# A late pair of normalisations behind the first GELU, and a split of x moved behind two tiles, in a conditional MLP

## The reference

```python
out_nr  = gelu(x @ w1_nr  + b1_nr)  @ w2_nr  + b2_nr      # condition 0
out_tsr = gelu(x @ w1_tsr + b1_tsr) @ w2_tsr + b2_tsr     # condition 1
h = gelu(x @ w1_sr + b1_sr)                               # condition 2, hidden size 1024
h = gelu(h @ w2_sr + b2_sr)
out_sr = h @ w3_sr + b3_sr
y = x + where(c == 0, out_nr, where(c == 1, out_tsr, where(c == 2, out_sr, 0)))
return (y - mean(y)) * rsqrt(var(y) + 1e-5) * gamma + beta
```

## Time and profile before

| | us |
|---|---|
| median of three runs | 562.37 (561.03 to 562.45) |
| the profiled execution's own time | 561.57 |
| span of the profiled execution | 559.8 |
| PE busy | 549.4 (98%) |
| POOL, DVE, ACT busy | 254.6, 267.7, 213.1 |
| DMA | 61.27 MB, mean 109 GB/s |

### The profile page before, as it was taken

One profiled execution on the slowest core, in us unless ns is written; L12 is line 12 of the kernel. 1 busy time (PEld: TensorE's weight loads), 2 busy tenths in 40 slices (PEclk: granted clock), 3 DMA queues, 4 the chain that ended last, 5 costly groups with the idle time before them and its releaser, 6 DMA issues. The chain is left out here.

```text
span 559.8 us, 8281 instructions
## 1 busy us (share of the span) xinstructions
PE 549.4 (98%) x2423; PEld 452.4 (81%) x2424; DVE 267.7 (48%) x417; ACT 213.1 (38%) x328; POOL 254.6 (45%) x225
## 2 busy tenths in 40 slices
PE   9999999999999999999999999999999999999994
PEld 6878887888888888888888888888888888888883
DVE  5661174865955856113610468212866105501656
ACT  5451335254253454214421452424255124513351
POOL 0879998575675576300430046700175300430056
PEclk9999999999999999999999999999999999999999
DMA  8875404444353443300330034400144200410032
GB/s 304 337 250 184 152 6 143 154 150 154 111 185 140 160 150 119 106 0 0 116 108 0 0 144 156 150 0 0 75 150 148 77 0 28 146 51 0 0 134 92
DMA packets 26225, 61.27 MB, mean 109 GB/s; under 512 B 3042, under 2 KB 3042, under 8 KB 26082
## 3 DMA queue, kind: packets, MB, share of 16 engines
q1 hardware_dynamic: 26208, 61.10, 31.2%
q10 hardware_dynamic: 2, 0.00, 0.0%
HBM read 44.31 MB, written 16.78 MB: 109 GB/s over the span
## 5 line engine op out<-in xcount | busy, mean ns | idle before, releaser
L456 DVE TENSOR_TENSOR g_lo<-bank,g_hi 128x512 fp32r<-128x512 f32 x112 | 77.4, 691 | 252.8 <-DVEq L117 252.8
L406 ACT ACTIVATE g_hi<-bank,bcol 128x512 fp32r<-128x512 f32 x112 | 77.8, 694 | 161.4 <-ACTq L117 160.2
L596 POOL TENSOR_TENSOR y<-y,row 128x512 f32<-128x512 f32 x64 | 95.2, 1507 | 51.0 <-POOLq L117 50.6
L600 POOL TENSOR_SCALAR var_eps<-mv 128x2 f32<-128x2 f32 x30 | 6.5, 218 | 227.6 <-POOLq L117 227.5
L428 ACT ACTIVATE y<-y,rstd 128x512 f32<-128x512 f32 x63 | 42.2, 717 | 172.0 <-ACTq L117 172.0
L236 PE MATMUL bank<-w_hi,g_hi 128*128 128x512 f32 x256 | 99.8, 390 | 1.2 <-PEq L117 1.2
L238 PE MATMUL bank<-w_hi,g_lo 128*128 128x512 f32 x256 | 99.7, 389 | 0.0
L237 PE MATMUL bank<-w_lo,g_hi 128*128 128x512 f32 x256 | 99.7, 389 | 0.0
L236 PE MATMUL bank<-x_hi,w_hi 128*128 128x512 f32 x240 | 93.5, 390 | 0.0
L237 PE MATMUL bank<-x_lo,w_hi 128*128 128x512 f32 x240 | 93.4, 389 | 0.0
L238 PE MATMUL bank<-x_hi,w_lo 128*128 128x512 f32 x240 | 93.4, 389 | 0.0
(11 more groups left out here) (42 smaller groups left out, 597.2 us busy)
## 6 DMA issues: line engine op xcount, KB each, us to landing
y<-x SPq DMA_DIRECT2D x64, 256.0 KB, 3.6
out<-y SPq DMA_DIRECT2D x64, 256.0 KB, 2.5
stage<-x_t SPq DMA_DIRECT2D x31, 512.0 KB, 3.3
w_raw<-weights SPq DMA_DIRECT2D x17, 512.0 KB, 4.7
row<-rows SPq DMA_DIRECT2D x1, 1280.0 KB, 11.4
stage<-x_t SPq DMA_DIRECT2D x2, 256.0 KB, 3.8
w_raw<-weights SPq DMA_DIRECT2D x2, 256.0 KB, 4.2
cond_sb<-cond ACTq DMA_DIRECT2D x1, 0.1 KB
```

The lines of the kernel that those rows point to most:

```text
L406: eng.activation(g_hi[:, slot, :], psum, ACT.Gelu, bias=b)
L456: eng.tensor_tensor(g_lo[:, slot, :], psum, g_hi32[:, slot, :], ALU.subtract).then_inc(s_gs, 1)
L596: eng.tensor_tensor(y[:, t, :], y[:, t, :], row[:, kind, :], ALU.add).then_inc(s_xb, 1)
L600: eng.tensor_scalar(var_eps[:, t:t + n], mv[:, t:t + n, 1], EPS, None, ALU.add).then_inc(s_var, n)
```

## The change

On ACT, the normalisations of tiles 2 and 3 no longer end the body of their own batch. They are done in the next batch, after the GELUs of its first hidden chunk. A register `turn` makes exceptions: batch 0 still does all four itself, and nothing is left over for batch 1. The last batch does what batch 14 left and its own three. `s_acc` is now counted for every kind, and PE takes four of them in a batch with no MLP.

On DVE, the second half of `x_lo` is made after tiles 0 and 1 instead of before them. On PE, SR takes `s_x23` in its first hidden chunk before x chunk 2, six matmuls in; NR did so before; TSR still takes it at its start. On SP, the first batch's rows 0 and 1 are loaded ahead of the x halves of batch 1, rows 2 and 3 behind them.

```diff
--- before.py
+++ after.py
@@ -195,11 +195,13 @@
                 load_pair(item)
             eng.dma_start(row[:, :, :].rearrange("p r h -> p (r h)"), rows.rearrange("r h -> (r h)").partition_broadcast(P)
                           ).then_inc(s_rows, 16)
+            load_row(0, 0)
+            load_row(0, 1)
             for f in range(2):
                 take(eng, s_stage[f])
                 load_x(x_halves[2 + f], f)
-            for t in range(TT):
-                load_row(0, t)
+            load_row(0, 2)
+            load_row(0, 3)
             landed = POOL_FIRST + POOL_ALL
             for item in POOL_ALL:
                 eng.wait_ge(s_loaded[landed[landed.index(item) - 2]], 16)
@@ -240,6 +242,9 @@
             def layer1(kind, j):
                 dst, n = bank[hidden_bank(kind, j)][:, :], bass.ts(j % HC, P)
                 for c in range(HC):
+                    if kind == SR and j == 0 and c == 2:
+                        take(eng, s_x23, 2)
+                        x_taken(1)
                     w = W1[kind] + HC * (j // HC) + c
                     sums = product(dst, w_hi[:, w, n], w_lo[:, w, n], x_hi[:, c, :], x_lo[:, c, :], c == 0, c == HC - 1)
                 sums.then_inc(s_h, 1)
@@ -317,9 +322,11 @@
                     return
                 take(eng, s_x01, 2)
                 x_taken(0)
-                take(eng, s_x23, 2)
-                x_taken(1)
+                if kind != SR:
+                    take(eng, s_x23, 2)
+                    x_taken(1)
                 if kind == NONE:
+                    take(eng, s_acc, 4)
                     read_next()
                     return
                 if kind == TSR:
@@ -410,22 +417,51 @@
                 take(eng, s_full[f], 16)
                 eng.copy(x_hi[:, 2 * f:2 * f + 2, :], stage[:, f, :, :]).then_inc(s_hi, 1)
 
-            def body(kind, read_next, last):
+            def normalise(t):
+
+                take(eng, s_v)
+                eng.sem_inc(s_acc, 1)
+                take(eng, s_rstd)
+                eng.activation(y[:, t, :], y[:, t, :], ACT.Copy, scale=rstd[:, t:t + 1]).then_inc(s_n, 1)
+
+            def body(kind, read_next, b):
+
                 read_next()
                 for j in range(n_hidden(kind)):
                     gelu(bank[hidden_bank(kind, j)][:, :], j % 4, B1[kind] + j)
+                    if j == 0:
+                        normalise_late(b)
+                if kind == NONE:
+                    normalise_late(b)
                 if kind == SR:
                     for i in range(HC):
                         gelu(bank[i][:, :], i, B2[SR] + i, (1, 1, 2, 0)[i])
-                if not last:
+                if b is not END:
                     split_x(0)
                     split_x(1)
-                for t in range(FINISHED_BY_OTHERS_END if last else TT):
-                    take(eng, s_v)
-                    if kind != NONE:
-                        eng.sem_inc(s_acc, 1)
-                    take(eng, s_rstd)
-                    eng.activation(y[:, t, :], y[:, t, :], ACT.Copy, scale=rstd[:, t:t + 1]).then_inc(s_n, 1)
+                normalise(0)
+                normalise(1)
+                if b is END:
+                    normalise(2)
+                    return
+
+                with eng.If_cmp(turn, 0, "IS_EQ"):
+                    normalise(2)
+                    normalise(3)
+                eng.reg_add(turn, turn, 1)
+
+            END = NBATCH - 1
+            turn = eng.alloc_register("turn_Activation")
+            eng.reg_mov(turn, 0)
+
+            def normalise_late(b):
+                if b is END:
+                    normalise(2)
+                    normalise(3)
+                else:
+                    with eng.If_cmp(turn, 2, "IS_GE"):
+                        normalise(2)
+                        normalise(3)
 
             eng.dma_start(cond_sb[:, 0:NBATCH], cond.rearrange("(a b) -> a b", a=1)).then_inc(s_cond, 16)
             eng.wait_ge(s_power, 1)
@@ -446,8 +482,8 @@
             eng.wait_ge(s_const, 16)
             cond_of = first_condition(eng)
             with eng.Fori(0, NBATCH - 1) as b:
-                batch(eng, cond_of, b, lambda kind, read_next: body(kind, read_next, False))
-            batch(eng, cond_of, NBATCH - 1, lambda kind, read_next: body(kind, read_next, True))
+                batch(eng, cond_of, b, lambda kind, read_next: body(kind, read_next, b))
+            batch(eng, cond_of, END, lambda kind, read_next: body(kind, read_next, END))
 
         @block.vector
         def _(eng):
@@ -504,9 +540,10 @@
                 read_next()
                 hidden(kind)
                 split_x(0, s_x01, 2)
-                split_x(1, s_x23, 2)
                 eng.wait_ge(s_rows, 16)
                 for t in range(0, TT, 2):
+                    if t == 2:
+                        split_x(1, s_x23, 2)
                     residual(kind, t)
                     residual(kind, t + 1)
                     stats(kind, t)
```

## The result

The changed kernel takes 583.54 us (median of six runs, 581.49 to 584.51) against 561.5 (median of six, 561.03 to 562.45): a ratio of 1.038, 95% interval 1.037 to 1.039, so 22 us slower. The forecast was slower too, but 576.9 with a range to 582.0; it moved by 14.5 where 22 was measured. One execution of experiment 8 (798.23 us, mean granted clock 0.655) ran in a slow state and is left out of its ratio.

What follows compares the result with a forecast made beforehand. PE, busy 98% of the span, was taken as the bound. Waits for x_lo and late GELUs, less 2.6 us won, summed to +14.5 us; on 562.37 this gave 576.9 us, range 571.0 to 582.0.

Steps and rivals of the forecast that it cites:

- Bound and gain: PE, busy 98% of the span, bounds the kernel; its gaps and waits of 2.6 us are all the change can win.
- x_lo behind SR batches: PE waits for x_lo's second half: 2.8 us each before two TSR batches, 1.4 each in two SR batches.
- 0.1 for the signal: Part of the SR to TSR wait: 0.1 us from x_lo's end to PE's start.
- TSR to SR: Batches 8 and 11: x_lo is ready at the boundary, PE wants it 1.36 us later; no cost.
- SR to NR: 24 matmuls, 5.4 us, lie ahead of PE's need for x_lo's second half; no cost.
- Late GELUs in NR: Deferred normalisations delay chunks 1 and 3 in six NR batches; PE loses 0.95 us each, 5.7 in all.
- Batch 7: NR to TSR: late stores and reloads delay tile 1's residual by 0.5 us; PE waits 1.2 us for x_lo.
- Batch 1: Batch 0 to batch 1 (SR): residual 1 at 25.2, x_lo ready at 30.2; PE waits 1.7 us.
- NR to SR: Batch 13: PE waits 0.1 us for x_lo's second half, bounds 0 and 0.5.
- rival 4: The clock falls after PE's five pauses of 1.4 to 2.8 us, costing 1.8 each: 586 us, chance 0.03.
- The added branches "at zero": On ACT, the added compare and branch were counted at zero because its queue runs ahead; at most 0.25 us per batch.

Runs made afterwards that it cites:

- experiment 8: The kernel before with only SP's order of the first rows changed (rows 0 and 1 ahead of x for batch 1): 562.05 us.
- Experiment 2: The changed kernel with ACT's order put back (all four normalisations at the end of their own batch): 575.73 us.
- experiment 3: The changed kernel with ten filler bf16 matmuls into bank 0 while a TSR batch waits for x's second half: 581.64 us.
- experiment 4: The changed kernel with TSR taking x's second half where SR does, six matmuls in: 577.2 us.
- experiment 6: The kernel before with a never-taken block of four normalisations on ACT in the bodies of all kinds but NR: 564.58 us.
- experiment 5: The kernel before with a never-taken block of four normalisations on ACT in every kind's body: 561.84 us.
- experiment 1: The changed kernel with DVE's order put back (both halves of x_lo ahead of the tiles): 571.68 us.
- experiment 11: The kernel before with leftovers only from batches 0 and 1, done behind the first GELU pair in SR and all four in NR: 565.24 us.

## Why the prediction was wrong

**Bound and gain: right.** PE was the bound, 2.6 us were all that could be won, and they went as described, though the GELU at 36.87 did not stay where I put it (39.81).

**x_lo behind SR batches: right.** 2.89 and 1.53 per wait against 2.7 and 1.3 before the 0.1 for the first matmul; the chain from tile 1's residual to x_lo's end was 5.0 us, as forecast. In sum 9.2 against 8.4: the term that was too small is "0.1 for the signal", the step from x_lo's end to PE's start, which measured 0.29 (336.09 to 336.38). TSR to SR and SR to NR cost nothing, as said.

**Late GELUs in NR: right.** 0.94 each against 0.95, at the first uses of chunks 1 and 3. (The forecast's own terms, 0.83 and twice 0.08, make 0.99.)

**Batch 7: mechanism right, size off.** 2.0 against 1.2. The step was "tile 1's residual 0.5 later than now": it starts 19.3 us into batch 6 instead of 18.0, so 1.3 later. Experiment 2, with the deferral undone, leaves 0.3 of the 2.0. Batch 1 was the same kind of error (residual at 25.7, not 25.2): 2.5 against 1.7. That one also varies: experiments 2 to 4, with the same order on DVE, lost 1.6, 2.5 and 2.3 there. With NR to SR (0.5 against 0.1) and the 0.8 of the SR terms these sizes add up to 2.8 us, nearly all inside their bounds.

**The clock: wrong, and this is what carried the result out of the range.** The step that failed is in rival 4: "The granted clock stayed full for the 4.9 us up to 557.3, with PE idle ... so pauses of 2.8 should not reach it". One tail is one sample: over the thirteen profiles the clock fell 2.0 us (experiment 6) to 5.3 us (experiment 5) after PE's last matmul had ended, and the kernel before's 5.0 was near the upper end. In the changed kernel the clock was at half level 2.1 us after PE's last matmul ended (28.76 to 30.9), while the same 2.9 us pause ahead of batch 10 passed unpunished and that ahead of batch 15 did not. The mechanism was among the rivals, at 3%, and priced at 1.8 for each of five pauses; it measured 1.6 for each of two in the profiled execution, and how much of it an execution has can differ (experiment 2). The forecast's own sign of being wrong, matmuls more than 0.23 apart in steady work, came true. The median lies 1.4 above the profiled execution; the other executions have no trace, and two of them, at the same mean granted clock of 0.991, took 583.32 and 583.75, so that 1.4 stays open. Without those stretches the profiled execution would have been near 579, inside the range. The gaps of 1.0 and 1.4 us from which I argued brought no fall in any profile, and neither did any pause that lost up to 2.2 (experiment 4). Of the nine unfilled pauses that lost 2.4 to 4.3 in the changed kernel and in experiments 1, 2, 3, 6 and 11, eight had a half-clock stretch begin in them or at most 1.5 us behind them.

**The added branches "at zero": right in NR batches, wrong in kind.** The branch itself costs nothing that shows, but with the added code the jump at the end of batch 0 stopped ACT once, for 2.8 us. In the changed kernel that is hidden; without the x_lo wait it was 3.3 more on PE and a fall of the clock (experiment 1). I had weighed instructions, not their places.

## What to carry to other kernels

When PE is the bound and the waits are read from a trace, give each new pause two prices: its length, and what the clock takes afterwards; here those that lost up to 2.2 us had no second price, and filling a pause with matmuls to a free bank saved it in the one trace that can tell (batch 15 of experiment 3). An idle engine has its idle time at a place: work moved from where ACT idled to where PE waits for it costs its full length, although ACT is idle for 63% of the span. Where a program branches on data, code that never runs can still make a jump stop the engine for 3 us, so compare the first pass of each engine over its jumps when a body grows.

## What the runs showed that was not expected

- One program ran at mean granted clocks of 0.988 to 0.997, and took 576.46 to 572.15 us (experiment 2).
- Half-clock stretches were 3.4 or 6.8 us long, with matmuls 0.43 us apart; they also began while PE was still idle.
- The clock stayed full behind a pause of batch 15 that ten filler matmuls (2.36 us) filled, and the program's median was 1.9 us lower than without them (profiled executions: 0.4).
- After PE's last matmul the clock stayed full for 2.0 to 5.3 us, one figure from each of thirteen profiles.
- ACT's jump at the end of batch 0 took 2.82 to 3.67 us in six of the thirteen programs and 0.40 or 0.41 in the others; in later batches it was 0.11 to 0.22 in all of them.
